# One reciprocal per image in the attention stage of a two-stage vision transformer layer

## What is computed

```python
att = jax.nn.softmax(jnp.where(causal, q @ k.T * 0.25, -inf), axis=-1)
y = att @ v                         # per image and head
y = y.transpose(0, 2, 1, 3).reshape(Bx, Tx, Cx)
y = y @ w_proj + b_proj
```

## Time and profile before

| what | before |
|---|---|
| median of 3 runs | 2326.57 us (2326.23 to 2331.97) |
| profiled execution: own time / span | 2324.15 us / 2322.4 us |
| PE, PEld busy | 92%, 89% of the span |
| DVE, ACT, POOL busy | 68%, 47%, 68% |
| granted TensorE clock, mean | 0.968 |
| attention stage | from the start to about 1336 us |

### The profile page before, as it was taken

How to read it: one execution, slowest core, us unless ns; L and a number is a source line. 1 busy time by engine, 2 the same in 40 slices (tenths; PEclk the granted TensorE clock), 3 DMA queues, 4 the chain that set the end, 5 groups by cost and what they waited for, 6 DMA issues and landing times. The chain is left out here.

```text
span 2322.4 us, 49007 instructions
## 1 busy us (share of the span) xinstructions
PE 2134.6 (92%) x14772; PEld 2068.0 (89%) x14772; DVE 1578.2 (68%) x4286; ACT 1084.3 (47%) x2850; POOL 1577.8 (68%) x2317
## 2 busy tenths in 40 slices
PE   5999999999999999999999479999999999999980
PEld 5999999999999999999988379999999999999980
DVE  5577777777777777777777446666666666665656
ACT  2444444444444444444444245454545445454545
POOL 3366767676767676767656657777777777777756
PEclk8999999999999999999999689999999999999995
DMA  7656565656565656565644143201010101001338
GB/s 204 144 132 146 132 145 130 145 129 145 129 145 130 142 130 142 128 144 128 144 97 99 32 107 56 42 5 29 4 31 5 30 5 29 4 4 24 56 44 334
DMA packets 235842, 223.54 MB, mean 96 GB/s; under 512 B 90647, under 2 KB 216066, under 8 KB 234688
## 3 DMA queue, kind: packets, MB, share of 16 engines
q1 hardware_dynamic: 135872, 147.40, 25.0%
q10 hardware_dynamic: 45568, 59.31, 11.2%
q0 software_dynamic: 54272, 15.20, 5.4%
HBM read 154.56 MB, written 98.38 MB: 109 GB/s over the span
## 5 line engine op out<-in xcount | busy, mean ns | idle before, releaser
L1159 POOL DMA_INDIRECT x_tokens<-yout,e_entry x240 | 383.6, 1598 | 182.5 <-DVE yout L1340 136.1
L668 PE MATMUL Y<-p,vp 128*102 128x198 f32 x1536 | 360.9, 344 | 14.8 <-ACT ysb L490 8.8
L1355 DVE TENSOR_TENSOR a<-UP,gate 128x384 f32<-128x384 f32 x320 | 178.5, 558 | 220.2 <-ACT gate L1295 214.7
L446 POOL DMA_INDIRECT expert_lists<-entry,slot x256 | 290.3, 1134 | 54.1 <-issue 54.1
L495 ACT ACTIVATE p<-ST 128x396 f32<-128x396 f32 x384 | 190.9, 497 | 261.3 <-PE ST L640 254.8
L1144 POOL DMA_INDIRECT rows<-x_wide,e_entry x240 | 249.5, 1040 | 78.8 <-issue 71.9
L1295 ACT ACTIVATE gate<-GT 128x384 f32<-128x384 f32 x320 | 157.8, 493 | 298.2 <-PE UP L1237 298.2
L141 POOL TENSOR_TENSOR word_p<-word_p 1x1 f32<-1x1 f32 x416 | 89.1, 214 | 294.0 <-ACT p L497 282.1
L412 POOL TENSOR_TENSOR x_lo<-x,x_hi 128x396 fp32r<-128x396 f32 x192 | 205.4, 1072 | 80.9 <-ACT x_hi L466 79.2
L668 PEld LDWEIGHTS Y<-p,vp 128*102 128x102 f32 x1536 | 221.7, 170 | 29.6 <-issue 8.8
L841 DVE TENSOR_REDUCE rm<-S 128x2 f32<-128x256 f32 x384 | 161.8, 421 | 106.5 <-PE S L659 104.0
(11 more groups left out here) (212 smaller groups left out, 6640.8 us busy)
## 6 DMA issues: line engine op xcount, KB each, us to landing
x<-in_xt ACTq DMA_DIRECT2D x180, 198.0 KB
q<-qk_features SPq DMA_DIRECT2D x384, 74.2 KB
k<-qk_features SPq DMA_DIRECT2D x192, 148.5 KB
qk_features<-qk_hi SPq DMA_DIRECT2D x96, 198.0 KB, 2.8
qk_features<-qk_lo SPq DMA_DIRECT2D x96, 198.0 KB, 3.8
rb<-rd ACTq DMA_DIRECT2D x128, 74.2 KB
t_x<-x_tokens SPq DMA_DIRECT2D x15, 576.0 KB, 8.2
out<-t_o ACTq DMA_DIRECT2D x15, 576.0 KB, 8.2
```

The source lines that it names most:

```text
L446: pool.indirect_dma_start(d["lists"][:, :], bass.IndirectOffsetOnAxis(ap=slot[o][0:REAL[t], t, c:c + 1], axis=0), entry[o][0:REAL[t], t, c ...
L668: return pe.matmul(Y[0:VW1, 0:TI], v0, p32[b][:, hh, 0:TI], start=start, stop=stop)
L1159: pool.indirect_dma_start(d["x1"][:, :], row_of(cc, t), yout[q][:], None, bounds_check=N - 1, oob_is_err=False, compute_op=ALU.add)\
L1355: dve.tensor_tensor(a32[m % 2][:], UP[m % 2][:, 0:TILE3], gate[m % 2][:], ALU.mult)\
```

## The change

`ysb` gets a place for each image and group (four in place of two). For group 0 of an image no reciprocal is taken. Instead ScalarE issues, in step 3 or 9, a DMA that copies the six rows of sums of group 0 to rows 102 to 107 of `ysb[:, im, 1]`, directly below the sums of group 1 (rows 96 to 101). The reciprocal of group 1 (step 5 or 11) then runs over twelve rows; in step 6 or 0 ScalarE issues two spreading DMAs one after the other, one for each group; and in step 8 or 2 VectorE makes both `y` of the image. The reciprocal also waits for the landing of the first copy (`s_dn`). The copy into `ysb` may now run four groups ahead of `y` and not two.

```diff
-        ysb = sb("ysb", [P, 2, TI], F32)
-        rd, rb = sb("rd", [P, 2, TI], F32), sb("rb", [CH, 2, TI], F32)
+        ysb = sb("ysb", [P, 2, 2, TI], F32)
+        rd, rb = sb("rd", [P, TI], F32), sb("rb", [CH, 2, TI], F32)
...
-                        wait(act, s_ym, u - 1)
+                        wait(act, s_ym, u - 3)
                         act.wait_ge(s_pv, (i - 1) * STEPS + (s - LAG_PV))
-                        act.activation(ysb[0:VW1, grp, :], Y[0:VW1, 0:TI], ACT.Copy).then_inc(s_yc, 1)
+                        act.activation(ysb[0:VW1, im, grp, :], Y[0:VW1, 0:TI], ACT.Copy).then_inc(s_yc, 1)
...
-                        act.wait_ge(s_rd, u + 1)
-                        src = rd[CH:VW1, grp, :].unsqueeze(1).broadcast_to([NH // 2, HD, TI])
-                        act.dma_start(rb[:, grp, :], src).then_inc(s_rb[grp], 16)
+                        v = (i - back) * 2 + im
+                        if grp == 0:
+                            act.wait_ge(s_yc, v * 2 + 1)
+                            wait(act, s_rd, v - 1)
+                            act.dma_start(ysb[VW1:VW1 + NH // 2, im, 1, :], ysb[CH:VW1, im, 0, :]).then_inc(s_dn, 16)
+                        else:
+                            act.wait_ge(s_rd, v + 1)
+                            for n in range(2):
+                                at = CH if n else VW1
+                                src = rd[at:at + NH // 2, :].unsqueeze(1).broadcast_to([NH // 2, HD, TI])
+                                act.dma_start(rb[:, n, :], src).then_inc(s_rb[n], 16)
...
-                        grp = j // 3
-                        dve.wait_ge(s_rb[grp], ((i - back) * 2 + (im + 1)) * 16)
-                        dve.tensor_tensor(y[im][0:CH, grp, :], ysb[0:CH, grp, :], rb[:, grp, :],
-                                          ALU.mult).then_inc(s_ym, 1)
+                        for grp in range(2) if j // 3 else ():
+                            dve.wait_ge(s_rb[grp], ((i - back) * 2 + (im + 1)) * 16)
+                            dve.tensor_tensor(y[im][0:CH, grp, :], ysb[0:CH, im, grp, :], rb[:, grp, :],
+                                              ALU.mult).then_inc(s_ym, 1)
...
-                        wait(dve, s_ym, u - 1)
-                        dve.wait_ge(s_yc, u + 1)
-                        dve.reciprocal(rd[CH:VW1, grp, :], ysb[CH:VW1, grp, :])\
-                            .then_inc(s_rd, 1)
+                        if j // 3:
+                            v = (i - back) * 2 + im
+                            wait(dve, s_ym, v * 2)
+                            dve.wait_ge(s_dn, (v + 1) * 16)
+                            dve.wait_ge(s_yc, v * 2 + 2)
+                            dve.reciprocal(rd[CH:VW1 + NH // 2, :], ysb[CH:VW1 + NH // 2, im, 1, :]).then_inc(s_rd, 1)
```

More of the change, by code:

```diff
@@ L285, in attention_block @@
         s_yc, s_rd, s_ym = sem("y_copied"), sem("reciprocal_ready"), sem("y_ready")
+        s_dn = sem("first_sums_moved")
         s_rb = [sem("reciprocal_spread0"), sem("reciprocal_spread1")]
@@ L503, in body @@
                         grp = j // 3
-                        u = (i - back) * 4 + (im * 2 + grp)
-                        act.wait_ge(s_rd, u + 1)
-                        src = rd[CH:VW1, grp, :].unsqueeze(1).broadcast_to([NH // 2, HD, TI])
-                        act.dma_start(rb[:, grp, :], src).then_inc(s_rb[grp], 16)
+                        v = (i - back) * 2 + im
[9 more added lines that the diff above has]
+                                act.dma_start(rb[:, n, :], src).then_inc(s_rb[n], 16)
                     if s == 0 and 1 in stages:
```

## The result

| | median | runs |
|---|---|---|
| before | 2326.4 us | 2318.52 to 2331.97, 4 runs |
| after | 2365.6 us | 2361.21 to 2366.94, 4 runs |

The ratio is 1.0168, with a 95% interval of 1.0135 to 1.0200: slower by 1.7%. The forecast was 2363.9 us. The profiled execution took 2366.94 us, 42.8 us more than the one before; the span is 2365.2 us.

A forecast was written before the change was run, and what follows sets the result against it. ScalarE's stream was taken to set TensorE in two stretches: 0.79 + 0.41 = 1.20 us a body, 34.8 us over 29 bodies, plus 2.5 us on 2324.15, plus 2.4 for the median: 2363.9 us; range 2338 to 2380 us.

The forecast's parts named there:

- What bounds the kernel: TensorE, 92% busy, waits for ScalarE's full stream in steps 0 to 2 and 6 to 8 of each body.
- step 0: Second spreading issue delays ScalarE's stream up to `ysb` of step 2, and TensorE with it: +0.79 us a body.
- step 6: Reciprocal ends 0.38 us earlier, the second issue adds 0.79 us, so `ysb` of step 8 comes later: +0.41 us a body.
- the rest of the run: Outside the 29 full bodies, the last bodies and the final spreading were estimated at 2.5 us together.
- The lateness of QK0: Steps 0 to 2: QK0 projection about 0.6 us late, hidden behind the exp's 0.79 us.
- The second issue: Second spreading DMA on ScalarE in steps 0 and 6, taken at 0.79 us, bounds 339 ns and 1.6 us.
- The rival of a cheap second issue: Second spreading issue costs only 0.34 to 0.45 us, giving 2336 to 2343 us; chance 0.12.
- the wait for the maxima: Step 7: TensorE's 0.35 us wait for VectorE's row maxima would be gone or nearly.
- Worth 0: Removed reciprocals, the moved `y` and the copy of the sums change nothing; twelve-row reciprocal taken at 1.39 us.
- The landing: Second spreading copy has 6.6 us until the second `y` of step 8 wants it; wait taken as 0.
- the rival: Second copy lands late, up to 1.8 us a body more, 2364 to 2416 us; chance 0.08.
- The last `y`: Last pair, where nothing hides the latency: TensorE's 8.78 us idle time gets 0.8 us longer.

The follow-up runs named there:

- the reordered one: Changed kernel, all DMAs on ScalarE, with the DMA of the maxima moved to just before the load of `x` and `x_hi` of step 1 behind `ysb`; 2347.0 us.
- the doubled one: Kernel before plus a second copy of the spreading DMA on ScalarE in steps 0 and 6, into a spare tile; 2435.6 us, ratio 1.0505.
- from other rows: Kernel before with the spreading DMA doubled on ScalarE, the spare copy reading six rows of a constant table; 2410.5 us, ratio 1.0376.

## Why the prediction was right

**What bounds the kernel** held. The two stretches in which TensorE waits for ScalarE are those in which all 1.28 us of the body arose: 0.70 us in steps 1 and 2, 0.58 in steps 7 and 8.

**How close it came** has luck in it. The mechanism held, but the terms missed both ways: -0.09 us in step 0, +0.17 in step 6, +3.2 us in the rest of the run. The profiled execution got 42.8 us longer and 37.3 were forecast; that the medians lie 1.7 us from the forecast comes also from the profiled execution after being the slowest of its four.

**Step 0, forecast +0.79, measured +0.70.** Shown from three sides: without the second issue on ScalarE (second spread on SyncE, or one spread only) the stretch is back at 6.36 us, and with nothing of the change but a second issue it is 7.05. The 0.1 us that is missing is the slack between ScalarE's stream and the chain through QK0. The lateness of QK0, which I had called hidden behind that of the exp, shows as a wait of its own (0.38 us for `h`, then 0.31 for the exp), within the same 0.70 us. The rule of the Trainium skill, "Trainium Kernel Development and Optimization", section "Key Constraints", that issuing from several engines only saves the sequencer's issue time, agrees for this stretch: that time was what mattered, and the move to SyncE gave back all of it. In steps 7 and 8 the same move gave back 0.26 of 0.58 us.

**The second issue, taken at 0.79 us, measured 0.75 to 0.76.** The rival of a cheap second issue fell. The Trainium skill, "Perfetto Trace Analysis", section "DMA Instruction — HWDGE (DVE, Sync)", counts a lock wait into the window of an issue; here next to none of it was saved (0.04 us) when the next issue of the same queue followed directly.

**Step 6, forecast +0.41, measured +0.58.** The step holds, its terms are each a little off. The reciprocal came 0.27 us earlier in the step and not 0.38 (734.04 against 714.30, with step 6 beginning at 733.80 against 713.79): after the maxima it starts 0.59 us behind the second reduction, where `y` had started 0.48 us behind it. `nm` came 0.53 us later, as 0.79 - 0.27 gives. Behind it the issue for `x` took 0.62 us in this body (0.52 in the median of 24) and not 0.34, which I had left out; the exp of step 7 came 0.67 us later. I had said that the wait for the maxima would be gone or nearly; it went from 0.35 us of TensorE's idle time to 0.34 us of its weight load's, which is 0.27 us earlier. And this doesn't shorten step 7, because the step now ends with a wait for that exp: it takes 4.36 us in place of 4.32. With one spread only, or both on SyncE, it takes 4.05.

**Worth 0**: the twelve-row reciprocal (1.39 us), the copy of the sums and its landing, the later `y`. The kernel with one spread has them all and a body of 38.60 us, 38.90 less 0.30.

**The landing** of the second copy was never late in the loop; the rival fell. `y` waited once, for 3.9 us near the end of the stage, where the kernel before had waited 4.2 and 0.6. In that rival the 1.3 us by which `y` would miss `PR0` went into the sum as 1.0; with 1.3 its upper end would be some 9 us higher, and no chance hangs on it. The Trainium skill, "DMA: Bandwidth & Descriptors", section "Why a DMA increments its semaphore by 16 and not by 1", would have the two copies on the same six DMA engines; no view here shows single engines. That the issues of `x` last longer behind a second copy would go with it, and doesn't show it.

**The rest of the run** was forecast at +2.5 us and is 42.8 - 37.1 = 5.7. The last `y` kept TensorE idle for 9.40 us in place of 8.78, +0.6 where 0.8 was forecast. By the starts of the instruction that runs once per body, 2.2 us have arisen before its first (129.2 us, 127.0 before), 3.1 us between its last three, behind the full bodies, and 0.4 us after its last. The start of the first lies between 126.8 and 130.3 us over all kernels, and at 127.7 us in the changed kernel with SyncE's spreads held back, so those 2.2 us may be scatter. For what remains I have no separate experiment.

**What stays open.** Why an issue behind spreading copies lasts longer. Counted from the first copy's issue, the issue for `x` ends 4.03, 3.94 and 4.03 us later in the bodies shown of the changed kernel, of the one with spreads held back and of the reordered one, 5.29 and 5.10 with the doubled one, and 4.91 us from other rows; behind the single copy on SyncE it ends 2.94 us later (716.90 + 0.84 - 714.80). That SyncE's spreads of `q` are not needed for it is shown. That it's the copies, and that the issue lasts until they are far enough along, is argued: it takes one more copy, and other source rows change it. What holds the issue up isn't known. The doubled kernel has three excesses over the changed one: 0.8 us a body of half clock, some 0.45 us in step 7 from reading the same rows, and 0.27 us of the later reciprocal. That leaves some 0.9 us of step 7 without a cause.

## What to carry to other kernels

A low busy share does not make an engine's issues free. Look at the stretch in which the bound engine waits for it: if the engine's stream is full there, each DMA issue in it (0.75 to 0.80 us here for a copy within on-chip memory) goes nearly whole onto the path (0.70 us in steps 1 and 2), and a queue with idle time in that stretch takes it off again, in part or whole. Merging two operations is worth what the path sees of it (8 us here, of 89 us of reciprocals removed), so count the issues that the merge adds at the same place before counting the busy time that it removes. And look at the granted clock before pricing a wait of TensorE: in the doubled kernel the half-clock stretches behind it cost 0.8 us a body on top. And when a stream and a second chain end together, shortening one gives nothing until the other is cut too: here the link to cut was one rounding ahead of a copy that everybody waited for.

## What the runs showed that I had not expected

A DMA issue has no fixed length. The load of `x` takes 0.34 us to issue in most places, but 0.62, 0.85, 1.48 and 1.85 us right behind two spreading copies, 0.84 us behind a single one that the other queue had issued, and `nm` took 1.42 us in place of 0.80 when two copies were issued by two queues at once. It was so before the change too: SyncE's six spreads of `q` took 3.83 us beside a spreading copy and 2.64 away from it. Where I moved such an issue earlier, it did not end earlier.
